# A six-layer attention kernel on one core: feed-forward work one turn later, in a new order on every engine

## The reference, cut to what matters

```python
# x: 16 items of 128 tokens x 128 features; all in float32
x = x + tanh(g0) * cross_attention(layernorm(x), ctx)
y = layernorm(x)
for i in range(6):                                   # DEPTH
    t = shift_tokens(y)                              # half of the features, one token later
    q, k, v = split(t @ Wqkv[i], 3)                  # 16 heads of 64
    q, k = rotary(l2norm(q) * q_scale[i]), rotary(l2norm(k) * k_scale[i])
    sim = 8 * q @ k.T    # in windows of 32: a window sees itself and the one before
    y = softmax(sim masked to the band) @ v @ Wo[i] + y
    t = shift_tokens(y)
    a, gate = split(layernorm(t) * g + b @ W1[i] + b1[i], 2)
    y = (a * gelu(gate)) @ W2[i] + b2[i] + y
return x + tanh(g1) * y
```

## Time and profile before

| | |
|---|---|
| time, median of 3 runs (lowest to highest) | 1667.87 us (1664.49 to 1669.25) |
| profiled execution, first to last instruction | span 1664.0 us |
| PE / DVE / ACT / POOL busy | 92% / 82% / 72% / 69% of the span |

### The profile page before, as it was taken

How to read it: one execution, slowest core, us unless ns; L and a number is a source line. 1 busy time by engine, 2 the same in 40 slices (tenths; PEclk the granted TensorE clock), 3 DMA queues, 4 the chain that set the end, 5 groups by cost and what they waited for, 6 DMA issues and landing times.

```text
span 1664.0 us, 79947 instructions
## 1 busy us (share of the span) xinstructions
PE 1529.5 (92%) x31136; PEld 1250.3 (75%) x31136; DVE 1370.9 (82%) x2593; ACT 1205.7 (72%) x2381; POOL 1155.7 (69%) x1118
## 2 busy tenths in 40 slices
PE   4579899999999999999999999999999999999996
PEld 2467777777777777877777777777777777777775
DVE  3578788888888888888888888888888888888883
ACT  3457777777777777777778777777777877777772
POOL 1276677777777777777677777777767766776770
PEclk8689999999999999999999999999999999999998
DMA  4101110111011011110111101112110001000001
GB/s 138 46 27 31 31 40 25 34 58 40 25 34 40 25 47 56 30 34 25 40 37 55 40 25 34 34 30 62 30 34 19 29 29 54 28 23 25 19 28 36
DMA packets 41455, 62.31 MB, mean 37 GB/s; under 512 B 3662, under 2 KB 30412, under 8 KB 41420
## 3 DMA queue, kind: packets, MB, share of 16 engines
q1 hardware_dynamic: 41420, 61.84, 12.6%
HBM read 18.84 MB, written 1.05 MB: 12 GB/s over the span
## 4 chain that ended last, share of the span: by engine, by line
PE 77%; ACT 10%; issue 6%; DVE 4%; POOL 1%; DMA 1%; DVEq 1%; SPq 1%; ACTq 0%; POOLq 0%
PE bank L1056 12%; PE bank L984 11%; PE bank L1068 10%; PE bank L1027 8%; PE bank L977 7%; PE bank L979 6%; PE bank L978 6%; PE bank L1103 4%; PE bank L1092 3%; ACT qT L542 3%; ACT v L556 3%; PE bank L1093 2%; PE bank L1094 2%; PE bank L1076 2%; ACT xfh L598 1%
## 5 line engine op out<-in xcount | busy, mean ns | idle before, releaser
L378 POOL TENSOR_TENSOR u<-u,t 128x512 f32<-128x512 f32 x384 | 489.3, 1280 | 194.9 <-DVE u L771 108.2
L392 POOL TENSOR_TENSOR u<-u,rn 128x512 f32<-128x512 f32 x384 | 392.4, 1042 | 7.9 <-ACT rn L536 1.1
L398 POOL TENSOR_TENSOR P<-P,rs 128x512 f32<-128x512 f32 x192 | 198.5, 1055 | 121.0 <-DVE rs L804 121.0
L977 PE MATMUL bank<-Wl,xsh 128*128 (+1 forms) x576 | 273.9, 476 | 5.7 <-DVE xsl L758 2.4
L771 DVE TENSOR_TENSOR u<-bank,TC 128x512 f32<-128x512 f32 x384 | 257.9, 681 | 1.5
L764 DVE TENSOR_REDUCE ss<-sq 128x8 f32<-128x512 f32 x384 | 244.5, 678 | 17.3 <-ACT sq L525 16.4
L780 DVE TENSOR_TENSOR t<-bank,TS 128x512 f32<-128x512 f32 x384 | 249.4, 680 | 2.2 <-issue 1.4
L525 ACT ACTIVATE sq<-bank 128x512 f32<-128x512 f32 x384 | 213.0, 595 | 31.8 <-DVE ss L764 20.5
L979 PE MATMUL bank<-Wh,xsh 128*128 (+1 forms) x576 | 229.5, 398 | 0.0
L978 PE MATMUL bank<-Wh,xsl 128*128 (+1 forms) x576 | 229.3, 398 | 0.0
L984 PE MATMUL bank<-shape_constants,u 128*128 128x128 f32 x1536 | 208.0, 273 | 5.7 <-POOL u L392 5.5
(11 more groups left out here) (102 smaller groups left out, 2949.6 us busy)
## 6 DMA issues: line engine op xcount, KB each, us to landing
vs<-v SPq DMA_DIRECT2D x96, 384.0 KB, 3.3
Wraw<-in_L_ffn_Wqkv_dram SPq DMA_DIRECT2D x72, 117.5 KB, 2.1
WoS<-in_L_ffn_Wo_dram SPq DMA_DIRECT2D x6, 512.0 KB, 3.7
W1h<-Wh SPq DMA_DIRECT2D x6, 341.0 KB, 2.5
W1l<-Wl SPq DMA_DIRECT2D x6, 341.0 KB, 2.9
Wraw<-in_L_ffn_W_dram SPq DMA_DIRECT2D x12, 116.0 KB, 2.1
OT<-in_x_dram SPq DMA_DIRECT2D x2, 512.0 KB, 5.6
v<-in_ctx_dram SPq DMA_DIRECT2D x2, 512.0 KB, 6.9
```

What stands on the lines that cost most here:

```text
L378: nc.gpsimd.tensor_tensor(u[:, r, c], u[:, r, c], t2[:, r, c % 2], ALU.add).then_inc(add_done[c], 1)
L392: nc.gpsimd.tensor_tensor(by_head(u[:, r, c]), by_head(u[:, r, c]), spread(rn[:, r, HC * c:HC * c + HC], HC, DH), ALU.mult).then_inc(qk_re ...
L977: nc.tensor.matmul(out, x[0], Wl[:, w], start=True, stop=False)
```

## The change

The loop gets a third lag (`LAST = 2`). The first part of a pair's work (x, chunks, v) keeps lag 0, the turns, scores and softmax move to lag 1 for both items, and all of the feed-forward work that follows `variance` on PE (and `residual` and what follows on DVE) has lag 2. All four lists are written in a new order, and `BANK_USERS` gives every product a new bank and a new user ahead of it. With these go the tables that say for the new order which use of a buffer comes ahead of which (`SQUARE_TURNS`, `SINE_BACK`, `QUERIES_BACK`, `KEYS_BACK`). `x_parts` and `x_rest` are made once per pair, on 256 columns, in place of once per item on 128. `second_values_bank` is gone: `values` waits for both of its banks itself. On SP the same transfers stand in another order. No arithmetic of any other step changes.

```diff
-LAST = 1
-SPLIT_LAG = 0
+LAST = 2
+HIGH_LAG, LOW_LAG = 0, 1
...
-        x_read = (v_full[0], v_full[0])
+        x_read = (ch_full[2], v_full[0])
...
         BANK_USERS = [
...
+            [("chunk", 1, 0, 0), ("up", 0, 0, 2), ("v", 1, 0, 0), ("chunk", 1, 1, 0)],
...
+            [("chunk", 0, 0, 0), ("turn_p", 0, 0, 1), ("chunk", 2, 0, 0), ("chunk", 3, 1, 0), ("turn_qk", 0, 0, 0), ("v", 0, 1, 0)],
...
+            [("turn_qk", 0, 1, 1), ("up", 1, 0, 2), ("down", 0, 0, 2), ("chunk", 0, 1, 0), ("v", 1, 1, 0)],
...
-                def x_parts(lag, r):
-                    n = (it - lag) * 2 + r
-                    act.wait_ge(h_ready, n_(it - lag) + 1)
-                    act.wait_ge(x_read[r], n_(n) - 1)
-                    nc.scalar.copy(xsh[:, r], shifted_x(it - lag, r)).then_inc(xsh_ready, 1)
+                def x_parts(lag):
+                    pair = it - lag
+                    act.wait_ge(h_ready, n_(pair) + 1)
+                    act.wait_ge(x_read[0], n_(pair * 2) - 1)
+                    act.wait_ge(x_read[1], n_(pair * 2))
+                    act.sem_inc(wait_met, 1)
+                    nc.scalar.copy(xsh[:], shifted_pair(pair)).then_inc(xsh_ready, 1)
...
-                def x_rest(lag, r):
-                    n = (it - lag) * 2 + r
-                    dve.wait_ge(xsh_ready, n_(n) + 1)
-                    nc.vector.tensor_tensor(xsl[:, r], shifted_x(it - lag, r), xsh[:, r], ALU.subtract).then_inc(xs_split, 1)
+                def x_rest(lag):
+                    pair = it - lag
+                    dve.wait_ge(xsh_ready, n_(pair) + 1)
+                    dve.sem_inc(wait_met, 1)
+                    nc.vector.tensor_tensor(xsl[:], shifted_pair(pair), xsh[:], ALU.subtract).then_inc(xs_split, 1)
...
-                def second_values_bank(lag, r):
-                    freed("values", 1, r)
-
                 def values(lag, r):
...
                     freed("values", 0, r)
+                    freed("values", 1, r)
```

More of the change, by code:

```diff
@@ new lines, in program, with square_place, squares_before @@
+            [("scores", 0, 1, 1), ("chunk", 3, 0, 0), ("turn_qk", 1, 0, 0), ("scores", 1, 0, 0)]]
+        SQUARE_TURNS = [(3, 1, 1), (2, 1, 1), (0, 1, 1), (1, 1, 1), (1, 0, 0), (0, 0, 0), (2, 0, 0), (3, 0, 0)]
+        SINE_BACK = [[1, 1], [1, 0], [0, 0], [0, 1]]
+        QUERIES_BACK = [[1, 0], [1, 0]]
+        KEYS_BACK = [[1, 0], [1, 0]]
+        def square_place(c, r):
+            return next(i for i, turn in enumerate(SQUARE_TURNS) if turn[:2] == (c, r))
+        def squares_before(c, r):
+            at = square_place(c, r)
+            turns, place = divmod(at - 2, len(SQUARE_TURNS))
+            before, of, lag = SQUARE_TURNS[place]
+            return before, of, SQUARE_TURNS[at][2] - lag + turns
@@ L620, in split_high @@
                     upper_part(pair + LAYER_PAIRS, pair % LAYER_PAIRS)
-                if on(0):
-                    x_parts(0, 0)
-                    x_parts(0, 1)
+                if on(1):
+                    norms(1, 0)
+                    square(3, 1, 1)
+                    square(2, 1, 1)
+                if on(2):
+                    o_out(1, 2, 1)
+                    o_out(0, 2, 1)
+                if on(1):
+                    square(0, 1, 1)
+                    square(1, 1, 1)
+                    keys(0, 1, 0)
+                    queries(1, 1, 0)
+                    queries(0, 1, 0)
+                    norms(1, 1)
+                    keys(1, 1, 0)
+                if on(2):
+                    deviations(2)
+                if on(0):
+                    x_parts(0)
+                if on(2):
+                    inverse_deviation(2)
+                if on(1):
+                    v_out(1, 1, 1)
+                if on(2):
+                    upper_x(2)
                 if on(1):
                     v_out(0, 1, 1)
+                    queries(0, 1, 1)
+                if on(0):
+                    square(1, 0, 0)
+                if on(1):
+                    keys(1, 1, 1)
+                    exp(1, 1, 0)
+                    exp(0, 1, 0)
+                if on(0):
+                    square(0, 0, 0)
+                if on(1):
+                    queries(1, 1, 1)
+                    keys(0, 1, 1)
+                if on(2):
+                    gelu(2)
+                if on(1):
+                    p_out(0, 1, 0)
+                    p_out(1, 1, 0)
                 if splitting:
@@ L852, in feed_back @@
                     i.then_inc(h_ready, 1)
+                if on(2):
+                    residual(2)
+                if on(1):
+                    straight(2, 1, 1)
+                    swapped(1, 1, 1)
+                    swapped(2, 1, 1)
                 if on(0):
-                    x_rest(0, 0)
+                    x_rest(0)
+                if on(2):
+                    normal(2)
                 if on(1):
+                    maxima(1, 1, 0)
+                    maxima(0, 1, 0)
+                if on(2):
+                    lower_x(2)
+                if on(1):
+                    minus_maxima(1, 1, 0)
+                    minus_maxima(0, 1, 0)
+                if on(0):
+                    straight(1, 0, 0)
+                    swapped(1, 0, 0)
+                if on(1):
+                    row_sums(1, 1, 0)
+                    row_sums(0, 1, 0)
+                if on(0):
+                    swapped(0, 0, 0)
+                    straight(0, 0, 0)
+                if on(1):
+                    maxima(0, 1, 1)
+                    minus_maxima(0, 1, 1)
                     maxima(1, 1, 1)
-                    maxima(0, 1, 1)
                     minus_maxima(1, 1, 1)
-                    minus_maxima(0, 1, 1)
+                if on(0):
+                    squares(1, 0, 0)
+                if on(2):
+                    gated(2)
+                if on(1):
                     row_sums(1, 1, 1)
```

292 lines of the change are left out of this document (116 added, 176 removed).

## The result

The changed kernel takes 1597.53 us (median of 4 runs, 1595.69 to 1600.49) where the kernel before takes 1667.36 on the same chip (4 runs, 1664.49 to 1669.25): ratio 0.9587, 95% interval 0.9566 to 0.9608. The profiled execution took 1600.49 us with a span of 1598.6.

A forecast was written before the change was run, and what follows sets the result against it. PE, busy 1529.5 of 1664.0 us, was taken as the bound. A turn's -0.95, kept as -0.9 over 46 turns (-41), and ends -3 + 2 gave -42: span 1622, median about 1626 us, range 1604 to 1664.

The forecast's parts named there:

- the turn's sum: Per turn on PE: idle time and overlap won, changes of kind and waits paid, -0.95 us, kept as -0.9.
- stops removed: PE's idle before the centring matmul, `up` and the second item's scores goes: 1.25 us a turn, plus 0.3 of overlap.
- new waits: PE waiting for ACT's v copies, `xfl` and the gelu in the new order: 0.3 us a turn, from 0 to 1.2.
- four more changes of kind: PE's groups of adjacent like calls rise from 30 to 34 a turn: 0.3 us more, from 0 to 0.6.
- lost overlap: Stops after a product on PE also lose overlap between matmuls, unlisted as idle: 0.3 us a turn, between 0 and 0.5.
- The 0.08: Price in us of each change of kind of work on PE, read from products (0.79 against 0.71); bounds 0 and 0.15.
- A tie, 0.1: PE's second product against ACT's copy of v tile 0: copy ends 3.9 us after variance, PE arrives at 3.86.
- sign of missed ties: PE waits for ACT's v or the gelu totalling over 0.5 would mean ties missed and the forecast too low.
- What costs nothing here: `x_parts` and `x_rest` once per pair, SP's new order and DVE's and POOL's load: 0, at most a tenth in the chain.
- Ends: Start of the run plus 2 us (-3 to +15), last turn's drain minus 3 (0 to -5).
- slower: ACT's v reads behind the feed-forward chain slide and stop PE twice a turn: 1680 to 1705 us, chance 0.12.
- The wait moves: Variance-to-`up` chain still ends last, extra changes eat the rest: 0 to -0.4 a turn, 1650 to 1668 us, chance 0.14.

The follow-up runs named there:

- The halves: Changed kernel with four of POOL's 128x512 operations a turn (two additions, two normalisations) each cut into two of 256 columns: 1574.47 us, ratio 0.9442.
- The kernel with two groups fewer: Changed kernel with PE's turning of P 0 moved up beside P 1, so two block projections also adjoin, in a turn's second half: 1604.86 us, ratio 0.9616.

## Why the prediction was wrong

The direction, the waits that go, PE as the bound, the clock in the middle and the place of the new wait were right. The span's gain was 65.4 us and not 42. The failed step is the turn's sum, "-1.25 - 0.3 + 0.3 + 0.3 = -0.95", by the sizes of its terms. The two that missed most are the stops removed and the new waits:

| term, us a turn | predicted | measured |
|---|---|---|
| stops removed | -1.55 | -2.02 |
| four more changes of kind | +0.3 | 0 (-0.04) |
| new waits | +0.3 | +0.66 |
| sum | -0.95 | -1.40 |

- *Stops removed.* The prediction took 1.25 from the list of waits and 0.3 for lost overlap. (The totals hold the long waits of the ends; in a turn of the middle the three listed times are 1.18.) By starts each of the three places costs 0.15 to 0.18 more than its listed time, and a fourth stop, before `values`, 0.34 by starts, was not counted at all: it is listed as 0.17, put down to "issue". All four went.
- *Changes of kind.* The 0.08 was read rightly between products and carried over to all kinds. A transpose behind transposes costs 0.08 more than a product there, so the two cancel. The kernel with two groups fewer is slower by 0.13 a turn because a transpose waits for POOL's division.
- *New waits.* The wait stands at the second product, as the prediction said ("A tie, 0.1"). It priced the chain as it stood in before, where POOL held up no instruction of it. The new order put POOL's additions of the second item beside `xsl`. The halves, which change nothing but the lengths of POOL's instructions, give back 0.35 at this place: a little over half of the 0.66 is the collision. The other 0.31 is the chain itself, for it stays when x is taken out of it altogether. This chain ran as forecast: with the halves `xfh` ends 3.38 after the start of variance and the copy 3.85 (forecast 3.38 and 3.9), and PE arrives at 3.80 (3.86). What the forecast left out is the hand-over. The copy of v tile 0 in the turn shown above for the halves, whose product starts at 742.40:

```profile
741.59 0.57 ACT L589 COPY v<-bank 128x512 f32<-128x512 f32 x1
```

The copy ends at 742.16, and the product starts 0.24 to 0.25 after the end of that copy in each of the eight kernels in which it waits for it. The prediction set the end of the copy against PE's arrival: a tie of 0.05, plus 0.25, is the 0.3. What in those links could be shortened was not tried. Its own sign of missed ties came (0.49 listed, 0.66 by starts, "over 0.5 together"), but the forecast was too high in time and not too low, since the stops removed were mis-sized by more.
- *"What costs nothing here": x once per pair.* In the old order true (1.0004), in the new one 6 us. DVE's idle 43 us of 320 are an average; the instruction stands in a chain and waits for another engine.
- *Ends.* The start costs 1.3 (predicted 2). After the last projection 2.5 are lost and not 3 won; the drain's lower clock was not foreseen. The shorter drain shows in the last turn instead, 28.0 us where before has 31.4.

Over the run: the turn's terms 0.45 x 47 = 21 us; the forecast kept 0.9 and 46 turns for 0.95 and 47, which is 3; the turns unlike the others, 6.6 before and 3.3 after, give 3; the ends take back 5. That is the 23 us between 42 and 65, but for 1. The other 5 us between 1626 and 1597.5 are no gain: the forecast put the median 3.9 above the span, and after's lies 1.1 below it.

Of the rivals, the "slower" one named the right engine and the right reads, behind the feed-forward's chain; they were late by 0.66 at one place, and not by 0.9 beyond the slack at two. "The wait moves" came true in part: 0.66 took the place of 2.02.

## What to carry to other kernels

Measure a stop from start to start against an equal place without one, and sum over all places: three listed waits told 1.25 us where 2.0 were to be had. When a new order puts VectorE's operations with two SBUF inputs beside GpSimd's work, look for the pairs that meet on a chain: move one of them, or cut GpSimd's instruction once, and stop before the pieces make GpSimd late. If exchanging two instructions only moves a stop, look at what both depend on, and at the length of each. And when a chain is laid against another engine's work, count the hand-over at its end: 0.25 us from ScalarE to TensorE and 0.30 from VectorE at the stops of the new order.

## What the runs showed that I had not expected

- A VectorE instruction with two SBUF inputs, 425 ns alone, took 1379, 830 and 554 ns beside GpSimd additions of 512, 256 and 128 columns; one with a PSUM input in the same place kept 470 to 480.
- Each further piece into which a GpSimd addition or normalisation of 512 columns is cut costs 0.14 us: from start to start 1.24 us whole, 2 x 0.69, 4 x 0.41 for the addition.
- Eight transposes in a row took 0.92 us, four and four between products 0.70, and no idle time was listed: of the 0.22, 0.13 is a wait for GpSimd that only the starts show, and 0.08 what the products save in exchange.
